# Row maxima of raw attention scores, taken for two heads at a time over two PSUM banks

## What is computed

```python
q = q * cos + _rotate_half(q) * sin            # 16 heads of width 32
k = k * cos + _rotate_half(k) * sin            # 4 key heads, each for 4 query heads
scores = jnp.einsum('bhqd,bhkd->bhqk', q, k) * scaling
attn = jax.nn.softmax(scores, axis=-1)
out = jnp.einsum('bhqk,bhkd->bhqd', attn, v)
```

## Time and profile before

| | |
|---|---|
| median of 3 runs | 1705.49 us (1704.61 to 1706.07) |
| the profiled execution | 1706.95 us |
| its span, first to last instruction | 1705.3 us |
| TensorE matmul busy | 1368.9 us, 80% of the span |
| VectorE busy | 759.1 us, 45% |
| ScalarE busy | 404.9 us, 24% |
| GpSimd busy | 424.6 us, 25% |
| mean granted TensorE clock | 0.84 of 2.4 GHz; 0.78 in the attention phase (190 to 1000 us) |
| largest group on VectorE | line 951, the row maxima |

### The profile page before, as it was taken

One profiled execution on the slowest core, in us unless ns is written; L12 is line 12 of the kernel. 1 busy time (PEld: TensorE's weight loads), 2 busy tenths in 40 slices (PEclk: granted clock), 3 DMA queues, 4 the chain that ended last, 5 costly groups with the idle time before them and its releaser, 6 DMA issues. The chain is left out here.

```text
span 1705.3 us, 23870 instructions
## 1 busy us (share of the span) xinstructions
PE 1368.9 (80%) x9120; PEld 843.2 (49%) x9120; DVE 759.1 (45%) x1633; ACT 404.9 (24%) x676; POOL 424.6 (25%) x455
## 2 busy tenths in 40 slices
PE   3094788879788788887978840499999999999994
PEld 2094452434426254352533430366666666666673
DVE  7982545455555656456455331332232222232231
ACT  2021123333333233333333410211111111111110
POOL 3000110100242223324233446122222222222221
PEclk8597675877969688696877965699999999999997
DMA  3022221323213242221323140888989989898882
GB/s 97 0 66 72 52 50 35 73 54 91 75 34 80 54 111 55 68 63 37 94 54 94 53 163 21 261 308 248 320 277 282 297 261 327 249 328 267 266 251 31
DMA packets 129837, 239.54 MB, mean 140 GB/s; under 512 B 58056, under 2 KB 64088, under 8 KB 129752
## 3 DMA queue, kind: packets, MB, share of 16 engines
q1 hardware_dynamic: 114232, 214.16, 40.4%
q0 software_dynamic: 15520, 24.22, 7.0%
HBM read 175.66 MB, written 38.90 MB: 126 GB/s over the span
## 5 line engine op out<-in xcount | busy, mean ns | idle before, releaser
L951 DVE TENSOR_REDUCE at_maxes<-at_ps 128x1 f32<-128x384 f32 x384 | 196.4, 553 | 131.3 <-PE at_ps L664 122.6
L808 ACT ACTIVATE bulk<-at_ps 128x1152 f32<-128x1152 f32 x128 | 144.9, 1132 | 367.4 <-PE at_ps L634 367.1
L1313 PE MATMUL mo_ps<-mo_x2s,mo_sgu 128*117 128x384 f32 (+1 forms) x1152 | 221.2, 344 | 0.0
L1313 PEld LDWEIGHTS mo_ps<-mo_x2s,mo_sgu 128*117 128x117 f32 (+1 forms) x1152 | 198.7, 181 | 13.4 <-issue 13.1
L1534 POOL DMA_INDIRECT out_rows<-mo_y,mo_scatter_ix x64 | 91.4, 1428 | 399.6 <-DMA out_rows<-mo_y,mo_scatter_ix 226.1
L664 PE MATMUL at_ps<-at_qb 32*128 32x384 bf16 x384 | 125.7, 442 | 78.6 <-DVE at_maxes L951 59.5
L1114 POOL DMA_INDIRECT slot_table<-at_toki,at_si x144 | 141.2, 981 | 51.0 <-issue 48.3
L664 PEld LDWEIGHTS at_ps<-at_qb 32*128 32x128 bf16 x384 | 28.6, 96 | 211.0 <-DVE at_maxes L951 173.5
L624 PE MATMUL at_ps<-WxT,at_xT 128*128 128x512 f32 (+1 forms) x576 | 114.0, 351 | 17.4 <-ACT at_v L853 15.6
L634 PE MATMUL at_ps<-at_QT 97*128 97x384 f32 x384 | 115.5, 416 | 6.9 <-ACT bulk L808 6.9
L1076 POOL TENSOR_TENSOR at_oTs<-at_oT,at_oTs 128x384 fp32r<-128x384 f32 x32 | 32.1, 1002 | 352.0 <-ACT at_oTs L820 352.0
(11 more groups left out here) (198 smaller groups left out, 1700.0 us busy)
## 6 DMA issues: line engine op xcount, KB each, us to landing
mo_wgu<-in_L_ffn_w_gate SPq DMA_DIRECT2D x32, 704.0 KB
mo_wgu<-in_L_ffn_w_up SPq DMA_DIRECT2D x32, 704.0 KB
bulk<-in_L_ffn_w_gate SPq DMA_DIRECT2D x32, 704.0 KB, 7.3
bulk<-in_L_ffn_w_up SPq DMA_DIRECT2D x32, 704.0 KB, 8.6
mo_wd<-in_L_ffn_w_down SPq DMA_DIRECT2D x32, 512.0 KB
bulk<-in_L_ffn_w_down SPq DMA_DIRECT2D x32, 512.0 KB, 5.4
at_QT<-at_qhi SPq DMA_DIRECT2D x64, 192.0 KB
rows_scores<-at_x SPq DMA_DIRECT2D x8, 864.0 KB, 3.7
```

The source lines that it names most:

```text
L808: A.activation(PT[:, N % RING, :, :], ps[:, 0:NT, 0:SEQ], ACT.Exp, scale=float(HD) ** -0.5)\
L951: V.tensor_reduce(maxes[:, s, h:h + 1], ps[:, 5 + u % 2, 0:SEQ], AX.X, ALU.max, negate=True)\
L1313: m = M.matmul(ps[0:SW[c], 5 + g, 0:SEQ], sgu[:, wa, g, k, SO[c]:SO[c] + SW[c]], x2s[:, xa, k, :], start=(k3 == 0), stop=(k3 == 3 * KC - 1))
```

## The change

The maxima are taken for a pair of units at once. TensorE waits ahead of the first raw matmul of a pair (u even) until the maximum of the whole last pair is done, then issues both matmuls, to banks 5 and 6, and only the second counts up `raw_scores`. VectorE waits for the pair and runs one `tensor_reduce` over `ps[:, 5:7, 0:384]`, which gives two columns of `maxes`, four apart (heads h and h + 4). The counts of `raw_scores` and `max_ready` are halved everywhere. In VectorE's slot two maxima of pairs come ahead of the second statistics and one behind, where there were three maxima of units ahead and three behind.

```diff
                 if u == HALF_UNITS:
                     pe.wait_ge(mrow_ready, 2 * a + 1)
-                wait(pe, max_ready, UNITS * a + u - 1)
+                if u % 2 == 0:
+                    wait(pe, max_ready, (UNITS * a + u) // 2)
                 rows = slice(HD * g, HD * (g + 1))
-                T.matmul(ps[:, 5 + u % 2, 0:SEQ], qb[rows, r, s * P:(s + 1) * P], qb[rows, REP, :],
-                         start=True, stop=True).then_inc(raw_scores, 1)
+                m = T.matmul(ps[:, 5 + u % 2, 0:SEQ], qb[rows, r, s * P:(s + 1) * P], qb[rows, REP, :],
+                             start=True, stop=True)
+                if u % 2 == 1:
+                    m.then_inc(raw_scores, 1)
...
-            def row_maximum(a, u):
+            def row_maxima(a, u):
+
                 half, s, r, g = unit(u)
-                dve.wait_ge(raw_scores, UNITS * a + u + 1)
+                dve.wait_ge(raw_scores, (UNITS * a + u) // 2 + 1)
...
-                V.tensor_reduce(maxes[:, s, h:h + 1], ps[:, 5 + u % 2, 0:SEQ], AX.X, ALU.max, negate=True)\
+                V.tensor_reduce(maxes[:, s, h:h + REP + 1:REP], ps[:, 5:7, 0:SEQ], AX.X, ALU.max, negate=True)\
                     .then_inc(max_ready, 1)
...
-                    for u in units[0:3]:
-                        row_maximum(a, u)
+                    for u in units[0:4:2]:
+                        row_maxima(a, u)
                     if prev and n == 9:
                         statistics2(c)
-                    for u in units[3:]:
-                        row_maximum(a, u)
+                    for u in units[4::2]:
+                        row_maxima(a, u)
```

More of the change, by code:

```diff
@@ L661, in raw @@
                     pe.wait_ge(mrow_ready, 2 * a + 1)
-                wait(pe, max_ready, UNITS * a + u - 1)
+                if u % 2 == 0:
+                    wait(pe, max_ready, (UNITS * a + u) // 2)
                 rows = slice(HD * g, HD * (g + 1))
-                T.matmul(ps[:, 5 + u % 2, 0:SEQ], qb[rows, r, s * P:(s + 1) * P], qb[rows, REP, :],
-                         start=True, stop=True).then_inc(raw_scores, 1)
+                m = T.matmul(ps[:, 5 + u % 2, 0:SEQ], qb[rows, r, s * P:(s + 1) * P], qb[rows, REP, :],
+                             start=True, stop=True)
+                if u % 2 == 1:
+                    m.then_inc(raw_scores, 1)
             def turn_maxes(a, half):
-                pe.wait_ge(max_ready, UNITS * a + HALF_UNITS * (half + 1))
+                pe.wait_ge(max_ready, (UNITS * a + HALF_UNITS * (half + 1)) // 2)
                 for s in range(NT):
@@ L677, in turn_x @@
                     wait(pe, mrow_ready, 2 * a)
-                    wait(pe, max_ready, UNITS * a)
+                    wait(pe, max_ready, UNITS * a // 2)
                 if k >= 2:
```

## The result

| | before | with the change |
|---|---|---|
| median of 4 runs beside each other, us | 1705.05 (1702.19 to 1706.07) | 1716.87 (1714.67 to 1720.3) |
| ratio | 1 | 1.0071, 95% interval 1.0054 to 1.0087 |
| the profiled execution (its span) | 1706.95 (1705.3) | 1715.8 (1713.8) |
| first raw matmul to first scores | 29.12 | 37.76 |
| mean granted TensorE clock | 0.840 | 0.831 |

The change makes the kernel slower by 0.71%, 12 us (9 to 15 by the interval). The profiled execution is one of the shorter ones.

What follows compares the result with a forecast made beforehand. The prediction took a loop of latencies between TensorE and VectorE, bare in the first stage, as the bound. Its terms, 7.7 + 0.55 + 0.33 - 1.2 = +7.4 us on the median of 1705.49, gave 1712.9 us, range 1702 to 1722.

Steps and rivals of the forecast that it cites:

- The new maximum: VectorE's one maximum over 2 x 384 elements: 0.95 us, where two ready old ones take 1.02 together.
- The raw pair: TensorE's two raw matmuls, the second no longer waiting: both done in 0.50 us at 1.2 GHz, next work after 0.43.
- The turn: One round of the bare loop (raw pair, hand-over, maximum, back to TensorE): 1.52 us in place of 1.147, +0.37.
- First stage: Maxima before any scores exist, nothing else running: +4.13 us in half one, +3.61 in half two, together +7.7.
- Slot 11: In each later stage, from VectorE's return from the division to the scores: 2.96 us in place of 2.64, +0.32.
- Slot 12: In each later stage, a wait of TensorE for VectorE: 1.95 us in place of 2.04, -0.09.
- Slot 15: In later stages, pairs following each other behind a late VectorE: scores +0.20 us later, +0.32 in the second stage.
- Slot 9: Around the second statistics: scores gain 1.8 us, most lost at the next raw pair, leaving -0.57 us.
- The steady passes: The five stages after the third: -0.24 us each, -1.2 together.
- the fourth rival: The pattern of clocks changes in each pass by 1 to 1.5 us, six times: 1705 or 1721; chance 0.13.
- slot 9 paying in full: Rival: six stages keep scores 1.8 us sooner, gaining 2.8 us each with the clock: 1699; chance 0.10.
- VectorE as the limit: Rival: VectorE bounds the kernel, so 192 cheaper maxima save 13 us: 1692; chance 0.03.

## Why the prediction was right, and where it was off

Forecast was 1712.9 us, slower with a chance of 0.78, the range 1702 to 1722; 1716.9 was measured. The sum was +7.4 us and the loss 12, so a good third of the loss is in no term as written; the width of the range covered that. The mechanism is the one named: where the coupling was taken away (four banks) the gain came out with the pairs in place, and where it was put in alone (single maxima) the loss was there. Pairs in the first stage alone cost 7.8 us on chip A.

- *The new maximum:* 0.95 predicted from lines 951 and 1018, 0.958 measured.
- *The raw pair:* both matmuls in 0.50 and the next work 0.43 later, as predicted.
- *The turn:* 1.52 predicted, 1.560 measured. The missing 0.04 is mostly the step from the pair's start to the maximum, 0.54 where I had put 0.51.
- *First stage:* +7.7 predicted, +8.64 measured. This term was mis-sized: 23 turns short by 0.04, and the difference is the whole of it.
- *Slot 11:* 2.96 predicted, 2.99. *Slot 12:* 1.95, 1.99. *Slot 15:* scores 2.96 after VectorE's return, 2.99. *Slot 9:* a gain of 0.57 predicted, 0.44 measured, and the scores ahead of it 1.7 us sooner where I had 1.8.
- *The steady passes:* the sum had -0.24 each; the text also held 102.40 unchanged to be possible, with a sum of 8.6, and that is what happened (102.21 to 102.40, against 102.33 to 102.40 before). The term of -1.2 us fell away. Its sign was not borne out either: from a stage's first raw matmul to the scores behind the pairs of slot 15 the change takes 0.17 us more in the fourth stage (516.62 - 465.78 = 50.84 against 505.62 - 454.95 = 50.67) and 0.20 to 0.24 more in the four after it.
- *What no term had:* 3.7 us in the third pass, where the sum had 0.33. The same pass took 103.25 us in an execution of the kernel before and 99.76 with waits by pairs throughout, so its length alone is no cost of a step of the change; and three subtractions more took 2.7 us off the second and third together. What makes the 4.3 us of those two passes stays open. I had named a changed pattern of clocks as the fourth rival, at 1 to 1.5 us a pass in six passes. If it is that, it came in one lump.

Of the rivals, slot 9 paying in full was wrong in the way that stood against it: the scores kept their 1.7 us only until the next raw pair. VectorE as the limit is refuted by its idle time, which grew to 155.5 us while its work shrank. The Trainium skill (VectorE: DVE Perf Modes, Rules for kernel authors) advises fewer VectorE instructions; here 192 fewer saved VectorE 12.4 us of busy time and the kernel nothing. Where VectorE was made the limit, in the first stage over four banks, that rule did pay, with 1.28 us of that stage for 24 instructions.

What stays open: the whole change costs 0.71% (0.54 to 0.87) in the result and 0.33% (0.18 to 0.48) on chip C, while its two halves cost 0.46% and 0.08% on chip A. The first stage's 8.6 us are the same in every trace of them; what returns or enlarges them afterwards, the changes of clock or something else, was not brought under control. And that the interleaved stages are free was shown only as they stand, in passes that kept their length.

The fastest versions are those with the first stage over four banks. In pairs there and single units later the ratio is 0.9958 and 0.9963 in two comparisons, 6 to 7 us faster than the kernel before (4 to 9 by the intervals). With single units throughout it is 0.9963, which cannot be told from it. None of them was measured beside the change.

## What to carry to other kernels

When two engines hand buffers back and forth, write down the turn of one buffer (fill, hand over, read, hand back) and how many buffers there are; in the four forms measured here the pace was the longer of the slowest engine's step and the turn divided by the buffers. Merging two reads into one instruction makes one buffer of two: here it turned 1.147 us a pair into 1.56 while every single instruction became as cheap as forecast. Look for the place where the loop is bare (a prologue, the first item of a pipeline), since that is where it pays or costs, and look there for memory that only later stages use.

## What the runs showed of the hardware that was not expected

The length of a pass is not the sum of its steps. In the traces of the result and of chips A and B the passes from the fifth stage on came back to 102.3 to 102.4 us whether the stage was walked in pairs or in units and even with 1.2 us of waiting added, with mean clocks of 0.78, 0.80 and 0.82. Then one such pass took 106.47 us. On chip C they alternated between 102.7 and 105.5 us. What holds a pass at one length was not isolated. In this loop 1.2 us more of waiting came out three times as nothing and once beside 4 us more, so a step of that size cannot be read from the length of a pass.
